# Cross attention's projection placed in the turned scores' second bank, and the expert weights loaded in sixteen parts

## What is computed

```python
# cross attention, for each of the 64 sequences
q = x @ Wq; k = context @ Wk; v = context @ Wv          # 16 heads of 8
attn = softmax(q k^T * hd**-0.5)                         # 128 x 77 per head
x2 = layernorm(x + (attn @ v) @ Wo)
# mixture: logits of 64 * 32 slots for each token
logits = x2 @ phi_w.T + phi_b
D = softmax(logits, axis=slot); C = softmax(logits, axis=expert)
X_tilde = sum over tokens of D * x2                      # "gather"
Y_tilde = tanh(norm(X_tilde)) @ expert_w + expert_b      # "experts", 64 matrices of 128 x 128
Y = sum over slots of C * Y_tilde                        # "mix"
```

## Time and profile before

| what | value |
|---|---|
| time, median of 3 runs (lowest, highest) | 1415.86 us (1413.57, 1416.15) |
| the profiled execution's own time | 1417.57 us |
| its span, first to last instruction | 1415.5 us |
| PE, PEld busy | 1300.1 (92%), 1060.9 (75%) us |
| DVE, ACT, POOL busy | 1109.7 (78%), 896.4 (63%), 1179.9 (83%) us |
| mean granted TensorE clock | 0.973 |
| kept_logits stores: count, size, median time to landing | 128, 256.0 KB, 2.0 us |

### The profile page before, as it was taken

One profiled execution on the slowest core, in us unless ns is written; L12 is line 12 of the kernel. 1 busy time (PEld: TensorE's weight loads), 2 busy tenths in 40 slices (PEclk: granted clock), 3 DMA queues, 4 the chain that ended last, 5 costly groups with the idle time before them and its releaser, 6 DMA issues. The chain is left out here.

```text
span 1415.5 us, 31661 instructions
## 1 busy us (share of the span) xinstructions
PE 1300.1 (92%) x11006; PEld 1060.9 (75%) x11006; DVE 1109.7 (78%) x2462; ACT 896.4 (63%) x1670; POOL 1179.9 (83%) x1050
## 2 busy tenths in 40 slices
PE   4886789999999679999999999988999999999998
PEld 3664566766666457777777777757999999999997
DVE  4897466666666568888888888877999999999996
ACT  2797366666666456767676777645666666666664
POOL 7564577878787379999999999967999999999997
PEclk8898699999999999999999999999999999999999
DMA  5112243343433242122222122212323232222221
GB/s 165 41 44 62 79 140 117 110 130 104 124 109 103 65 130 83 75 82 75 83 75 82 75 82 76 80 49 75 100 70 101 75 95 84 86 86 83 87 82 31
DMA packets 77183, 123.61 MB, mean 87 GB/s; under 512 B 8353, under 2 KB 45794, under 8 KB 77026
## 3 DMA queue, kind: packets, MB, share of 16 engines
q1 hardware_dynamic: 75426, 117.16, 26.4%
q0 software_dynamic: 1088, 4.19, 1.0%
q10 hardware_dynamic: 512, 0.23, 0.1%
HBM read 70.28 MB, written 51.27 MB: 86 GB/s over the span
## 5 line engine op out<-in xcount | busy, mean ns | idle before, releaser
L987 POOL TENSOR_TENSOR gather_d<-gather_e,gather_rinv 128x1024 f32<-128x1024 f32 x128 | 244.8, 1913 | 44.3 <-DVE gather_rinv L966 44.3
L1246 POOL TENSOR_TENSOR mix_c<-mix_e,mix_rinv 128x1024 f32<-128x1024 f32 x128 | 240.9, 1902 | 18.8 <-DVE mix_rinv L1234 17.0
L1314 PEld LDWEIGHTS last_Y<-kept_phi,last_cT 128*128 128x128 f32 x2048 | 248.4, 192 | 7.3
L1314 PE MATMUL last_Y<-kept_phi,last_cT 128*128 128x128 f32 x2048 | 249.1, 275 | 0.0
L815 POOL TENSOR_TENSOR cross_kd<-first_pack,kept_consts 128x624 fp32r<-128x624 f32 x128 | 155.6, 1236 | 69.0 <-DMA first_pack<-first_halves 61.6
L1330 ACT COPY last_cT<-last_T 128x1024 f32<-128x1024 f32 x128 | 128.4, 1004 | 132.1 <-PE last_T L1321 132.1
L723 DVE TENSOR_REDUCE cross_mx<-cross_S 128x8 fp32r<-128x624 f32 x128 | 103.5, 809 | 122.0 <-PE cross_S L561 122.0
L1231 DVE TENSOR_REDUCE mix_sums<-mix_e 128x16 f32<-128x1024 f32 x128 | 155.8, 1217 | 34.3 <-ACT mix_e L1205 33.9
L962 DVE TENSOR_REDUCE gather_rsum<-gather_e 128x32 f32<-128x1024 f32 x128 | 156.1, 1220 | 26.6 <-ACT gather_e L935 26.6
L981 POOL TENSOR_TENSOR gather_dl<-gather_d,gather_dh 128x512 fp32r<-128x512 f32 x128 | 166.2, 1299 | 0.0
L924 ACT COPY gather_keep<-gather_L 128x256 f32<-128x256 f32 x256 | 94.7, 370 | 103.8 <-PE gather_L L898 96.9
(11 more groups left out here) (202 smaller groups left out, 3015.3 us busy)
## 6 DMA issues: line engine op xcount, KB each, us to landing
kept_logits<-gather_keep SPq DMA_DIRECT2D x128, 256.0 KB, 2.0
mix_read<-kept_logits SPq DMA_DIRECT2D x64, 512.0 KB, 3.7
first_halves<-first_qk SPq DMA_DIRECT2D x32, 412.0 KB, 3.1
first_pack<-first_halves SPq DMA_DIRECT2D x64, 128.0 KB
first_pack<-first_halves SPq DMA_DIRECT2D x32, 206.0 KB
first_pack<-first_halves SPq DMA_DIRECT2D x64, 78.0 KB
attn_xTg<-in_xT SPq DMA_DIRECT2D x16, 256.0 KB, 2.7
kept_xres<-in_x POOLq DMA_DIRECT2D x4, 1024.0 KB, 12.8
```

The costliest lines, as they stand in the source:

```text
L987: pool.tensor_tensor(dd[u % 4][:].rearrange("p i (n s) -> p i n s", n=16), e[u % 2][:], rinv[u % 2][:].rearrange("p (i n) -> p i n", i=2). ...
L1246: pool.tensor_tensor(self.cc[u % 2][:], self.e[u % 2][:], self.rinv[u % 2][:].unsqueeze(2).to_broadcast([128, 16, EXPERTS]), ALU.mult)\
L1314: ins = pe.matmul(psY[t % 2][:, 0:128], cT[u % 2][:, c, :], w.yk[:, 8 * (u % 2) + c, :], start=(u % 2 == 0 and c == 0), stop=(u % 2 == 1 a ...
```

## The change

The projection of sequence n goes to the first 128 columns of bank 1 of `psP` for n below 61, and to `psM` as before for the last three. There it waits for `e_low` (the exponentials of banks 0 and 1 in this step) in place of the reader of `psM`, it no longer takes `psM`, DVE's L730 reads it there, and `turned_scores`, which writes all four banks of `psP` anew, waits for `y_done` too. In the gather block the one load of the weights and the load of the biases before the stores are gone; after every eighth store SP issues a load of four of the 64 weight matrices (256 KB), sixteen in all, and the biases come after the last. The PE of `run_experts` waits for all sixteen.

```diff
+        def projection(n):
+            return banks[:, 1, 0, :] if n < B - 3 else psM[:, 0:128]
...
             def project(n):
                 pe.wait_ge(oT_ready, n + 1)
-                take_bank(y_done, n + 1)
-                pe.matmul(psM[:, 0:128], oT[n % 2][:], w.xo[:], start=True, stop=True).then_inc(pj_made, 1)
+                if n < B - 3:
+                    pe.wait_ge(e_low, n + 3)
+                else:
+                    take_bank(y_done, n + 1)
+                pe.matmul(projection(n), oT[n % 2][:], w.xo[:], start=True, stop=True).then_inc(pj_made, 1)
...
             def turned_scores(n):
                 r, b = n // 2, n % 2
                 reach(pe, e_ready, n)
+                reach(pe, y_done, n - 2)
                 reach(pe, xl_ready, n - 4)
...
-                dve.tensor_tensor(y[n % 2][:], psM[:, 0:128], w.xres[:, tokens(n)], ALU.add).then_inc(y_done, 1)
+                dve.tensor_tensor(y[n % 2][:], projection(n), w.xres[:, tokens(n)], ALU.add).then_inc(y_done, 1)
...
+    WE_EVERY, WE_PART = UNITS // 16, EXPERTS // 16
...
-            sync.dma_start(w.we[:], io["expert_w"].rearrange("n d h -> d n h")).then_inc(w.we_loaded, 16)
-            sync.dma_start(w.beT[:], io["expert_bT"]).then_inc(w.be_loaded, 16)
+            by_row = io["expert_w"].rearrange("n d h -> d n h")
             for u in range(UNITS):
                 sync.wait_ge(kept, 2 * u + 2)
                 sync.dma_start(w.kept[rows(u), u % 2], keep[u % KEEPS][:]).then_inc(stored[u % KEEPS], 16)
+                if u % WE_EVERY == WE_EVERY - 1:
+                    some = slice(u // WE_EVERY * WE_PART, (u // WE_EVERY + 1) * WE_PART)
+                    sync.dma_start(w.we[:, some, :], by_row[:, some, :]).then_inc(w.we_loaded, 16)
+            sync.dma_start(w.beT[:], io["expert_bT"]).then_inc(w.be_loaded, 16)
...
-            pe.wait_ge(w.we_loaded, 16)
+            pe.wait_ge(w.we_loaded, 16 * 16)
```

## The result

The changed kernel takes **1399.24 us** (median of 4 runs, 1398.43 to 1401.92 us), the kernel before 1415.34 us beside it (4 runs, 1413.57 to 1416.15 us): a ratio of 0.9879, 95% interval 0.9862 to 0.9896. The gain is 16.1 us where 10.5 us were forecast, and the time lies 2.6 us under the lower end of the range. The profiled execution took 1401.92 us; its span is 1399.9 us against 1415.5 us, so these two profiles differ by 15.6 us.

| stretch, us | before | after | difference |
|---|---|---|---|
| cross attention: end of the second maximum in step 0 to that in the last step | 151.15 to 467.89, 316.7 | 150.72 to 459.82, 309.1 | -7.6 |
| gather block: first PE matmul to DVE's first work of the experts | 485.7 to 936.2, 450.5 | 477.6 to 920.5, 442.9 | -7.6 |
| from there to the end | 479.3 | 479.4 | 0.1 |

The account below looks back on a forecast made before the run. PE was taken to bound the gather block except at its stalled start, and a chain through PE and DVE cross attention. Weights -7.2 and bank -3.3 sum to -10.5 us, forecast 1405.3 us, range 1401.8 to 1410.0 us.

Parts of the forecast that it names:

- Weights: Gather block start: ACT no longer waits for the first store behind the 4 MB load; -7.2 us.
- 5.71 + 1.53: Gather block: PE's unit 4 starts 5.71 us earlier, and 1.53 us of low clock after PE's idle time goes too.
- the 7.8 us that the prediction allowed: Gather block: upper bound of the gain from loading the weights in parts, 0.6 us above the forecast 7.2 us.
- Bank: Cross attention: turned maxima start without L730; 0.05 us in 59 steps plus 0.4 us for two steps, -3.3 us.
- The shift L580 needs the turned scores issued: Cross attention step: shift starts 0.43 us after the turned scores, at 305.96 us, later than ACT's copy L695 at 305.82 us.
- The bounds of 0.03 to 0.06 us: Cross attention: least and most a step was said to gain around the forecast 0.05 us.
- POOL and the SP queue have idle time in each pair of steps: Cross attention: this idle time pays for the shorter step, so everything after the shift moves forward; no cost in the sum.
- The weights alone: Cross attention: the bank gives nothing, only the gather block gains; -7.2 us, 1408.6 us; chance 0.11.
- The whole wait goes: Cross attention: `xl_ready` binds less, 61 steps gain 0.19 us each, 11.6 us in all; 1397.0 us; chance 0.04.
- The third wait: Cross attention: a third semaphore wait delays turned scores L572, 61 steps lose 11.6 us; 1420.3 us, slower; chance 0.03.
- Parts cost what the load hid: Gather block: sixteen DMAs take 32 us for 17.2 us, ACT waits the 14.8 us difference; 1420.1 us; chance 0.01.
- The stall only moves: Gather block: unit 4 waits for POOL or DVE, over half of 7.2 us and bank gain lost; 1413.5 us; chance 0.04.

Follow-up runs that it names:

- one late load: Changed kernel with the weights in one 4 MB load again, issued behind the store of unit 63 in mid gather block; 1408.23 us, one execution.
- ACT's queue: Changed kernel with the weights in one 4 MB load at the start of the gather block, issued by ACT on its own queue; 1398.24 us, one execution.
- the parts alone: Kernel before with the weights in sixteen parts and the projection left in psM; 1409.50 us, ratio 0.9935.
- the wait kept: Changed kernel with the turned maxima waiting for y_done again, projection still in bank 1 and free to go early; 1406.40 us, ratio 0.9915.
- the late scores before: Kernel before with the turned scores also waiting for rs_ready, DVE's reciprocal; 1416.88 us, one execution.
- the late scores after the change: Changed kernel with the turned scores also waiting for rs_ready, DVE's reciprocal; 1409.39 us, one execution.
- phi in parts: Changed kernel with phi loaded in sixteen parts of 64 KB, one per pair of steps, instead of one 1 MB load; 1393.92 us, repeated at 1394.05 us.

## Why the prediction was wrong in size and right in direction

**Weights: the right mechanism, forecast a little small.** Forecast -7.2 us (5.71 + 1.53), measured -7.6 us in the two profiles. The stall is gone, ACT is released by PE, unit 4 follows unit 3 by 3.21 us, and no half-clock stretch follows, since PE no longer stands. Unit 4 came 13.30 us after the first matmul (13.7 us forecast), as unit 2 started 6.89 instead of 7.33 us after it. Parts land in 2.9 us where 3.1 us were taken, delay no store by more than 0.3 us in the profile after, and their issue (0.435 us) was between the bounds. The experiments with one late load and with ACT's queue confirm the cause: the place behind the load on SP's queue. In the other runs the gather block took 450.9 and 451.3 us with the load in front and 441.9 to 442.6 us with sixteen parts, 8.2 to 9.4 us less, which is over the 7.8 us that the prediction allowed. ACT's wait for the first store was 7.8 and 7.7 us in those two kernels and 6.53 us in the one execution from which the forecast was read.

**Bank: the right wait, mis-sized.** The turned maxima start without L730, the next late thing for the turned scores is L746's successor L753, and they gain 0.05 us, all as forecast. The step that failed is "The shift L580 needs the turned scores issued (0.43 us later, 306.01 us before)". The 0.43 us were a distance seen in the timeline, taken for a duration: 0.28 us of it was issue, the rest, 0.15 us, was PE's wait for L695. With 0.30 us in its place the shift is at 305.53 + 0.30 = 305.83 us, and L695 at 305.82 us: 0.18 us a step, which is what was measured, and 60 steps of it are 10.8 us instead of 3.3 us. The two runs with a delayed start of the turned scores show this directly, and the run that kept the wait shows that nothing else in the bank edit gives the 0.18 us. The bounds of 0.03 to 0.06 us failed with it, since they varied the semaphore's way and not this number.

A smaller miss changed nothing: PE started L541 0.06 us after the maximum, not 0.12 us. The 0.12 us of the earlier trace rows was the way from the end of L730 (+0.19 us) to L538 (+0.31 us), and the way from the maximum is shorter. It changes nothing in the sum, as the shift is held by the turned scores either way: L702 ends 0.09 us before it.

The lower end of the range has a slip too: 1415.86 - 11.7 - 2.6 is 1401.6 us and not 1401.8 us, and the measured time is below both.

**What was not foreseen.** The changed kernel gives back 3.6 us in steps 6 and 7. The prediction said that "POOL and the SP queue have idle time in each pair of steps, which pays for the shorter step". This holds for the ordinary pairs; in the pair where SP loads phi, the store stands behind 1 MB, ACT already waited 1.48 us for it, and this wait grew to 3.02 us, with a stop of PE and a low clock behind it. The profiles with phi in one load fall into two groups by this pair. In the four where the turned maxima wait for L730 (the kernel before, the parts alone, the wait kept, the late scores before) it took 10.8 to 12.8 us, and ACT waited 1.05 to 1.69 us; in the seven where they don't, 13.8 to 15.8 us and 2.99 to 3.80 us. The means of the groups, 11.9 and 14.8 us, differ by 2.9 us, so the 3.6 us of the two profiles are one draw. A dip of the clock is not the mark of the change either: it came in all seven, but also with the wait kept and with the late scores before, after stops of PE of 1.81 and 1.28 us, and not in the kernel before after 1.47 us. The length of the step is not what decides, as the late scores after the change, with 4.963 us a step, had the 15.8 us.

A part of ACT's longer wait can be read. Counted from ACT's copy of the same kind a pair earlier, the store landed after 11.5 us in the kernel before and after 12.6 us in the kernel after (11.0 to 11.7 us and 12.5 to 13.3 us in the two groups), and a pair is 0.36 us shorter; together this is about the 1.54 us by which the wait grew. So that the bank edit brings this cost, and that phi in parts removes it, is shown. Why the store lands later, in 5.4 to 6.0 us instead of 4.6 to 4.9 us, stays open. Phi in parts on the kernel before, without the bank edit, was not tried.

Part of the forecast's nearness is luck. The bank was worth some 10.8 us in its steps where 3.3 us were forecast, and a cost that the forecast did not have took 3.6 us of that away again; with phi in parts, where this cost is gone, the time is 11 us under the forecast and not 6 us.

**The rivals.** *The weights alone* (0.11): falls, the bank gave more than forecast. *The whole wait goes* (0.04) has nearly the right size per step (0.19 us) and the wrong mechanism: `xl_ready` does bind, at +0.51 us as forecast, yet the step gains 0.18 us. Its 1397.0 us is 2.2 us under the measured time; it too left out the pair at phi. *The third wait* (0.03): the turned scores wait for three semaphores and start 0.05 us earlier; falls. *Parts cost what the load hid* (0.01): sixteen parts take 16 x 2.9 = 46 us under way where one load takes 17.2 us, but ACT waits for none. *The stall only moves* (0.04): it doesn't, as unit 4 follows unit 3 by 3.21 us.

The Trainium skill ("DMA: Bandwidth & Descriptors", Rules for kernel authors) asks for transfers of 1 MiB or more. The landing times agree with it in direction: 17.4 us for one load, 4 x 6.3 = 25 us for four, 46 us for sixteen. As advice for this place the trace disagrees: the one load in front of the stores cost 7.6 to 9.4 us, and the fragments cost nothing measurable, since the transfers lie beside PE's work. Parts of 1 MB satisfy the rule and remove the stall as well. The fit of the Trainium skill ("DMA: Bandwidth & Descriptors", Anatomy of one DMA), which is for DMAs issued by GpSimd, gives estimates of 11.6, 4.4 and 2.6 us for 4 MB, 1 MB and 256 KB; on SP's queue 17.4, 6.3 and 2.9 us were measured, and the measurement decides.

## What to carry to other kernels

A distance between two starts in a timeline is not a duration: before it goes into a sum, ask whether the second instruction was waiting for something else meanwhile, and read the starts of a merged group one by one. A large load on a queue that also carries stores on which a buffer depends can cost most of its landing time at the first store behind it, as it did here; put it behind them in parts, or on another queue. And when a loop gets shorter, look for the one iteration that does something extra: slack read from the ordinary ones says nothing about it, and there the gain can turn into a wait.

## What the runs showed of the hardware

- Sixteen matmuls of 32 rows and 128 columns on four row groups start within 0.27 us, while the row of the group has 0.50 us; the remaining 0.23 us, by ends that the profile models, lie beside the next group, which started 0.03 us after the last of them.
- The same sixteen in an order that uses two row groups at a time start over 0.49 us.
- A store of 256 KB on SP's queue took 2.0 us to land in the median, up to 4.3 us behind a load of 1 MB, and 15.2 us behind one of 4 MB; beside 4 MB on ACT's queue, up to 6.8 us. In one profile of the changed kernel stores with no load before them took up to 4.5 us. The store of 412 KB took 3.1 us in the median of the kernel before, and 4.6 to 6.0 us behind the 1 MB of phi.
- The DMA behind 4 MB on SP's queue held SP at its issue, 12.77 us for the biases and 10.98 us for a store, where a store otherwise takes 0.32 us to issue.
- A stop that grows can cost more than its growth: PE's at the phi load grew from 1.47 us (PE for DVE's L716) to 3.13 us, by 1.66 us, and the pair of steps by 3.6 us, with 0.61 of full granted over 8 us from 184 us on instead of 1.00. The clock over 175 to 195 us was 1.00 in the kernel before and with phi in parts, 0.83 and 0.91 in two profiles of the changed kernel, and 0.91 in the two kernels whose PE stopped there for 1.28 and 1.81 us.
